# A fused attention and mixture-of-experts block on one core: one masking product per score tile, one maximum and one exponent per tile, and several steps put in another order

## The chip, the cores and the metric

The kernel runs on one core of one Trainium2 chip. The metric is the time of one execution on the device in microseconds (us); lower is better. The engines are called PE (TensorE), DVE (VectorE), ACT (ScalarE), POOL (GpSimd) and SP (SyncE, which only issues transfers here).

## What is computed

`x` and `ctx_2048` are 32 sequences of 64 tokens with 256 features. One block of a network is applied to them, with two gates (cut):

```python
# attention: keys and values are the 64 context rows of the same sequence and 64 rows made of x
q, k_new, v_new = xn @ wq.T, xn @ wk.T, xn @ wv.T            # xn = layernorm(x)
k, v = concat([ctx, k_new]), concat([ctx, v_new])            # per sequence, 128 rows
attn = softmax(q @ k.T / sqrt(256)) @ v @ wo.T
x = x + tanh(g_xattn) * attn
# feed-forward on xf = layernorm(x), 2048 tokens, 8 experts of width 176, the best 2 of each token
probs = softmax(xf @ gate_w.T);  top_p, top_i = top_k(probs, 2)
y = sum over the two experts of top_p * proj_e(silu(fc1_e(xf)) * fc2_e(xf))
y = y + sigmoid(xf @ shared_gate.T) * shared_proj(silu(shared_fc1(xf)) * shared_fc2(xf))   # width 704
x = x + tanh(g_ffn) * y
```

All is in float32. The kernel splits each matmul operand into a high and a low half (`_hi`, `_lo`) and multiplies three pairs of halves, hi x hi, hi x lo, lo x hi. So ACT makes each high half (a copy) and DVE the low one (a subtraction), and only then may PE go on: PE, ACT, DVE, PE is the chain of nearly every step.

## The kernel before

The 2048 tokens are four chunks (`c` = 0 to 3, `LAST` = 3) of four tiles (`j` = 0 to 3) of 128 tokens, that is two sequences a tile. Every engine has its own program, a list of steps written out by hand in order; each engine goes through its list strictly, and semaphores join them. What stands ahead of a step on its engine therefore sets when it can start.

**Attention** (lines 641 to 682 on PE, 960 to 1000 on ACT, 1380 to 1425 on DVE). For tile j of chunk c PE does `scores(c, j)`: six products of 256 columns into bank 4 or 5. The 256 columns are the keys of both sequences of the tile, so that half of what is computed belongs to the other sequence. `row_max` on DVE takes the maximum of each half of the rows over the keys of their own sequence, in two instructions (`own_keys`), and `exps` on ACT does the same with two exponent instructions, each with an instruction that reads the sum; the other sequence's places in `PR` stay at the zeros that were written once at the start. Then come `values` (12 products), `probs_t` (two transposes), `probs_hi` and `probs_lo`, `v_hi` and `v_lo`, and `attend` (six products; the second waits for `v_lo`, the third for `probs_lo`), `residual` and `aggregate`. Between these stand the steps of the next chunk (`first_norm`, `project`: its queries and keys, in bank 3) and of the last ones (`second_norm`, `router`, `logits`; `two_best`, `counts`, `route` and `slots`, which find for each token and expert a place in the sorted list; `scatter` on POOL writes rows there).

For a chunk c > 1, `slots(c - 2)` stands on DVE between `residual(c, 0)` and `v_lo(c, 1)`, and reads what `route(c - 2)` put into bank 7. In chunk 0 `ln1_stats(2)` stands ahead of `v_lo(0, 0)`; it needs the third chunk of `x`.

**Start** (lines 603 to 620, 922 to 935, 1323 to 1347): constants and weights are loaded and split; PE runs 18 transposes of a constant (`warm`) between the first steps.

**Shared feed-forward** of chunks 0 to 2 (`fc`, `pj`) comes next, then the **experts**: 39 tiles of 128 sorted rows, in a loop written out (`e_step`).

**End** (lines 816 to 824, 1549 to 1558): the shared feed-forward of chunk 3 in six blocks, `fc` (12 products of 512 columns; six in block 4) and `pj` (12 products of 256 columns; eight in block 4), with `s_silu`, `s_mult`, `s_hi`, `s_lo` between them. Meanwhile the partial sums come back from memory, and `combine(0)` to `combine(7)` add them: 0, 2, 4, 7 on DVE, 1, 3, 5, 6 on POOL. `s_last` adds chunk 3's shared part, and results are stored. Chunk 2's partial sums are loaded last; `combine(6)` and `combine(7)` are theirs.

Of the kernel before, what the change touches and what calls it, by code (L numbers as in the profile page):

```python
# [111 lines left out]
def build(nc, x, ctx_t, wa, sw, ew, rw, gates, consts, rconsts, out):  # L112
    with ExitStack() as stack:
# [316 lines left out]
        def _(pe):  # L430
# [95 lines left out]
            def attend(c, j):  # L526
# [1222 lines left out]
```

## Time and profile before

| | |
|---|---|
| time, median of 3 runs (range) | 295.76 us (294.89 to 295.84) |
| the profiled execution: its time, its span | 294.28 us, 292.5 us |
| busy in the span: PE, DVE, ACT, POOL | 272.9, 213.9, 170.7, 136.1 us |
| start and attention | to about 114 us |
| shared feed-forward of chunks 0 to 2 | about 114 to 183 us |
| the 39 expert tiles | about 183 to 265 us |
| shared feed-forward of chunk 3 and the stores | 265 us to the end |

The span runs from the first to the last instruction; the time of an execution lies 1.8 us above it. PE's products are pipelined and their ends are modelled, so waits of PE are best read from the starts of its products.

### The profile page before, as it was taken

The numbers are of one execution on the slowest core, as the hardware profiler recorded it, in microseconds if no ns is written. First come the engines' busy times: TensorE is split into PE (matmuls) and PEld (weight loads), VectorE is DVE, ScalarE is ACT, GpSimd is POOL, SyncE is SP. The second block draws the span as 40 slices with busy tenths as digits, with TensorE's granted clock in tenths as the row PEclk, the third lists the DMA queues.
The fourth block names the chain that finished last, engine by engine and source line by source line (L and its number), as shares of the span: only waits on it lengthen the run. The fifth ranks groups of instructions, "written<-read, shape, count | busy, mean of one in ns | idle before, by whom it ended". The sixth has DMA issues, their size and how long they took to land.

```text
span 292.5 us, 5859 instructions
## 1 busy us (share of the span) xinstructions
PE 272.9 (93%) x1777; PEld 245.7 (84%) x1777; DVE 213.9 (73%) x694; ACT 170.7 (58%) x401; POOL 136.1 (47%) x161
## 2 busy tenths in 40 slices
PE   3998899999899899999999999899999999999992
PEld 3887789789778677888788888899999999998882
DVE  6867776979869759768776767868778777763285
ACT  2775678687566567473335446566666667654240
POOL 2420831441784427453450000068778778776141
PEclk9999999999999999999999999999999999999999
DMA  6470244221136112544425744368888888756796
GB/s 194 190 256 2 73 149 141 72 80 50 38 91 242 74 40 85 186 144 125 150 76 182 247 140 145 131 113 134 136 141 134 136 139 137 116 69 72 291 354 217
DMA packets 25022, 40.18 MB, mean 137 GB/s; under 512 B 2976, under 2 KB 18976, under 8 KB 24992
## 3 DMA queue, kind: packets, MB, share of 16 engines
q1 hardware_dynamic: 16272, 27.43, 29.1%
q0 software_dynamic: 7152, 9.57, 19.4%
q10 hardware_dynamic: 1568, 2.80, 2.7%
q8 instruction: 15, 0.25, 0.4%
q14 instruction: 15, 0.12, 0.2%
HBM read 22.68 MB, written 17.11 MB: 136 GB/s over the span
## 4 chain that ended last, share of the span: by engine, by line
PE 57%; DVE 23%; issue 7%; ACT 6%; DMA 3%; POOL 1%; SPq 0%; DVEq 0%; ACTq 0%; POOLq 0%
PE bank L437 43%; PE bank L702 8%; DVE ew_lo L1097 4%; DMA xn_all<-x_dram 3%; PE bank L801 3%; PE bank L755 3%; DVE work L1453 2%; ACT ew_hi L830 2%; DVE xt_lo L1097 2%; ACT sh_hi L830 2%; DVE neg_max L1145 2%; DVE sh_lo L1097 2%; DVE ln_stats L1108 1%; DVE work L1168 1%; ACT work L862 1%
## 5 line engine op out<-in xcount | busy, mean ns | idle before, releaser
L1650 POOL DMA_INDIRECT y_d<-work,dest_of_slot x39 | 60.5, 1552 | 56.2 <-DVE dest_of_slot L1504 54.7
L437 PE MATMUL bank<-ew_hi,xt_hi 128*128 (+2 forms) x172 | 53.9, 323 | 1.4 <-DVE xt_lo L1097 0.7
L437 PE MATMUL bank<-ew_lo,xt_hi 128*128 (+2 forms) x172 | 51.7, 301 | 0.0
L437 PE MATMUL bank<-ew_hi,xt_lo 128*128 (+1 forms) x133 | 40.5, 305 | 0.0
L1610 POOL DMA_INDIRECT xs_d<-xn_all,slot_of_pair x32 | 33.3, 1042 | 10.1 <-issue 7.3
L1097 DVE TENSOR_TENSOR xt_lo<-bank,xt_hi 128x256 fp32r<-128x256 f32 (+2 forms) x90 | 35.5, 397 | 3.2 <-ACT xt_hi L830 2.0
L437 PE MATMUL bank<-xt_hi,sw_hi 128*128 128x512 f32 x88 | 34.8, 395 | 0.2 <-DVE work L1453 0.2
L437 PE MATMUL bank<-xt_lo,sw_hi 128*128 128x512 f32 x88 | 34.5, 392 | 0.0
L437 PE MATMUL bank<-xt_hi,sw_lo 128*128 128x512 f32 x88 | 34.3, 390 | 0.0
L830 ACT ACTIVATE xt_hi<-bank 128x256 fp32r<-128x256 f32 (+1 forms) x90 | 32.7, 409 | 2.4 <-PE bank L801 1.1
L437 PEld LDWEIGHTS bank<-ew_hi,xt_hi 128*128 128x128 f32 (+1 forms) x172 | 32.4, 189 | 2.0 <-DVE xt_lo L1097 0.9
L437 PE MATMUL bank<-ew_hi 128*128 128x256 f32 (+1 forms) x100 | 30.8, 314 | 3.4 <-DVE ew_lo L1097 2.0
L437 PEld LDWEIGHTS bank<-ew_lo,xt_hi 128*128 128x128 f32 (+1 forms) x172 | 32.7, 190 | 0.1
L1097 DVE TENSOR_TENSOR ew_lo<-bank,ew_hi 128x512 fp32r<-128x512 f32 (+1 forms) x41 | 22.6, 580 | 13.2 <-ACT ew_hi L830 13.1
L830 ACT ACTIVATE sh_hi<-work 128x512 fp32r<-128x512 f32 (+1 forms) x24 | 15.2, 632 | 28.8 <-DVE work L1453 25.2
L437 PE MATMUL bank<-ew_hi,ew_lo 128*128 128x256 f32 (+1 forms) x100 | 30.4, 310 | 1.5 <-DVE ew_lo L1097 1.5
L437 PE MATMUL bank<-ew_lo,ew_hi 128*128 128x256 f32 (+1 forms) x100 | 29.7, 304 | 0.6 <-DVE ew_lo L1097 0.2
L702 PE MATMUL bank<-sw_hi,sh_hi 128*128 128x256 f32 x96 | 27.2, 289 | 0.3 <-DVE work L1468 0.2
L830 ACT ACTIVATE ew_hi<-bank 128x512 fp32r<-128x512 f32 (+1 forms) x45 | 21.6, 518 | 9.3 <-PE bank L437 8.2
L702 PE MATMUL bank<-sw_lo,sh_hi 128*128 128x256 f32 x96 | 26.6, 282 | 0.0
L437 PEld LDWEIGHTS bank<-ew_hi,xt_lo 128*128 128x128 f32 x133 | 25.1, 188 | 0.0
L1490 DVE TENSOR_TENSOR work<-work,bank 128x176 f32<-128x176 f32 x39 | 13.1, 337 | 16.0 <-ACT work L1025 16.0
(161 smaller groups left out, 678.8 us busy)
## 6 DMA issues: line engine op xcount, KB each, us to landing
work<-xs_d SPq DMA_DIRECT2D x39, 136.0 KB, 2.5
weight_stage<-ew_dram SPq DMA_DIRECT2D x10, 486.5 KB, 3.7
y_d<-work SPq DMA_DIRECT2D x6, 512.0 KB, 3.9
work<-ctx_t_dram SPq DMA_DIRECT2D x4, 512.0 KB, 3.3
ew_hi<-y_d SPq DMA_DIRECT2D x4, 512.0 KB, 8.1
ew_hi<-y_d ACTq DMA_DIRECT2D x4, 512.0 KB, 7.0
xn_all<-x_dram SPq DMA_DIRECT2D x3, 512.0 KB, 6.6
xs_d<-pad_row SPq DMA_DIRECT2D x9, 136.0 KB, 2.0
```

The costliest lines, as they stand in the source:

```text
L437: last = nc.tensor.matmul(dst, a, b, start=(n == 0), stop=(n == len(pairs) - 1))
L702: last = nc.tensor.matmul(B[4 + t][:, 0:D], h[:, t * P:(t + 1) * P], w, start=(j == 0 and n == 0), stop=(j == S_FULL and n == len(parts) - 1))
L755: last = nc.tensor.transpose(rows_bank(n)[:, k * P:(k + 1) * P], EX[:, w, k * P:(k + 1) * P], ident)
L801: last = nc.tensor.transpose(B[4 + v][:, i * P:(i + 1) * P], EH[:, v, i * P:(i + 1) * P], ident)
L830: return nc.scalar.activation(dst, src, ACT.Copy, scale=scale)
L862: nc.scalar.activation(XA[:, j, :], XNR[:, c * TPC + j, :], ACT.Identity, bias=nb1[:, j:j + 1], scale=rs1[:, j:j + 1]).then_inc(a_xn, 1)
L1097: return nc.vector.tensor_tensor(dst, src, hi.bitcast(F32), ALU.subtract)
L1145: last = nc.vector.tensor_reduce(nmx[r, j % 2:j % 2 + 1], own_keys(B[4 + j % 2], b), mybir.AxisListType.XY, ALU.max, negate=True)
L1453: nc.vector.tensor_tensor(SHF[0:rows, j % 2, :], STH[0:rows, j % 2, :], h2, ALU.mult).then_inc(v_h, 1)
L1490: nc.vector.tensor_tensor(EH[:, u % 2, 0:F_E], ETH[:, u % 2, :], B[2 + u % 2][:, F_E:2 * F_E], ALU.mult)
L1610: nc.gpsimd.indirect_dma_start(out=xs_d, out_offset=bass.IndirectOffsetOnAxis(ap=POS[:, i, n:n + 1], axis=0), in_=XN[:, n, :], in_offset=N ...
L1650: nc.gpsimd.indirect_dma_start(out=y2_d, out_offset=bass.IndirectOffsetOnAxis(ap=IX[:, n:n + 1], axis=0), in_=EY[:, n % 4, :], in_offset=None,
```

## The change

- **Scores.** A seventh product is added to each `scores`: `SIDES` holds ones where row and token are of the same sequence, `OTHERS` holds -1e28 at the keys of the other sequence. It adds a number far down to the scores of the other sequence and zero to the own ones. So `row_max` and `exps` are one instruction each over all 256 columns. Both tiles are written once at the start; the zeros of `PR` go.
- **Slots.** `slots(c - 2)` moves behind `aggregate(c, 0)`, `route(c - 2)` behind `attend(c, 1)` and, for chunks 0 and 1, into bank 4. `scatter` is put behind `rstd2` on POOL.
- **Chunk 2.** `attend(2, 2)` moves behind `project(3, 3)`, its `residual` behind `project_lo(3, 3)`.
- **Chunks 0 and 1.** `ln1_stats(2)` goes behind `row_max(0, 2)`, `project_lo(1, 0)` ahead of `residual(0, 0)`, and the two halves of `first_norm(2)` stand one ahead of each of the first two `scores` of chunk 1.
- **Start.** 13 warming transposes instead of 18; `weight_lo(2)` and `(3)` ahead of `ln1_stats(1)`; `cached_hi(0)` behind `project_hi(0, 0)`; the load of the router's weights later.
- **End.** `fc` and `pj` of chunk 3 in another order; `combine(6)` goes from POOL to DVE, and `combine(7)` ahead of `s_last`.

The diff, cut to its core:

```diff
+        SIDES = EW[0][:, 9216:9216 + P]
+        OTHERS = EW[0][:, 9216 + P:9216 + 3 * P]
...
@@ PE @@
                 if j == 0:
-                    waits += [(0, v_qk, 4 * c + 4), (0, g_ct, c + 1)]
+                    waits += [(0, v_qk, 4 * c + 4), (0, g_ct, c + 1), (0, v_far, 1)]
...
-                              for m in range(KD) for a, b in THREE], waits)
+                              for m in range(KD) for a, b in THREE] + [(SIDES, OTHERS)], waits)
...
-                if j == 1 and c > 1:
-                    waits = waits + [(0, v_pos, c - 1)]
...
-                bank, o = (B[1], 0) if c == LAST else (B[7], D)
+                bank, o = (B[1], 0) if c == LAST else (B[7], D) if c == LAST - 1 else (B[4], 0)
...
             first_norm(0, 0)
-            warm(4)
             first_norm(0, 1)
-            warm(4)
+            warm(3)
...
+                if c == 1:
                     first_norm(c + 1, 0)
+                    scores(c, 0)
                     first_norm(c + 1, 1)
+                    scores(c, 1)
...
                 values(c, 1)
-                if c > 1:
-                    route(c - 2)
...
                 attend(c, 1)
+                if c > 1:
+                    route(c - 2)
...
-                attend(c, 2)
+                if c != LAST - 1:
+                    attend(c, 2)
                 values(c, 3)
                 probs_t(c, 3)
                 if c < LAST:
                     project(c + 1, 3)
+                if c == LAST - 1:
+                    attend(c, 2)
...
             fc(LAST, 1)
+            pj(LAST, 0)
+            fc(LAST, 2)
+            fc(LAST, 3)
+            pj(LAST, 1)
+            fc(LAST, 4)
+            fc(LAST, 5)
             for j in range(2, S_BLK):
-                if j < S_FULL:
-                    pj(LAST, j - 2)
-                fc(LAST, j)
-            for j in range(S_FULL - 2, S_BLK):
                 pj(LAST, j)
@@ ACT @@
-                for b in range(2):
-                    r = slice(b * SEQ, (b + 1) * SEQ)
-                    last = nc.scalar.activation(PR[r, j % 2, :, b, :], own_keys(B[4 + j % 2], b),
-                                                ACT.Exp, bias=nmx[r, j % 2:j % 2 + 1], accum_out=den[r, j:j + 1])
-                last.then_inc(a_exp, 1)
+                nc.scalar.activation(PR[:, j % 2, :, :, :].rearrange("p x s n -> p (x s n)"), B[4 + j % 2][:, 0:2 * P],
+                                     ACT.Exp, bias=nmx[:, j % 2:j % 2 + 1], accum_out=den[:, j:j + 1]).then_inc(a_exp, 1)
...
             weight_hi(1)
-            cached_hi(0)
             weight_hi(2)
             weight_hi(3)
-            for i in range(4):
+            project_hi(0, 0)
+            cached_hi(0)
+            for i in range(1, 4):
                 project_hi(0, i)
-            first_apply(1, (0, 1))
...
-            first_apply(1, (2, 3))
+            first_apply(1)
@@ DVE @@
-                for b in range(2):
-                    r = slice(b * SEQ, (b + 1) * SEQ)
-                    last = nc.vector.tensor_reduce(nmx[r, j % 2:j % 2 + 1], own_keys(B[4 + j % 2], b),
-                                                   mybir.AxisListType.XY, ALU.max, negate=True)
-                last.then_inc(v_mx, 1)
+                nc.vector.tensor_reduce(nmx[:, j % 2:j % 2 + 1], B[4 + j % 2][:, 0:2 * P], AX_X, ALU.max, negate=True).then_inc(v_mx, 1)
...
+                far = nc.vector.memset(OTHERS.rearrange("p (x s n) -> p x s n", x=2, s=2)[r, :, 1 - b, :].bitcast(F32), FAR)
```

What DVE has around `slots(0)` in chunk 2 before (L1172 ends `residual(2, 0)`, L1259 to L1264 is `slots(0)`, the rows behind it are `v_lo(2, 1)`, `second_lo(1, 1)`, `probs_lo(2, 1)` and `project_lo(3, 1)`):

```order
L1172 BN_STATS ln2_stats<-work 128x6
L1259 TENSOR_TENSOR work<-work,bank7 128x32
L1260 TENSOR_REDUCE work<-work 128x4
L1259 TENSOR_TENSOR work<-work,bank7 128x32
L1260 TENSOR_REDUCE work<-work 128x4
L1261 TENSOR_SCALAR payload<-work,tanh_gates 128x4x2
L1262 SCALAR_TENSOR_TENSOR slot_of_pair<-work 128x2x4
L1264 COPY work<-work 128x8
L1097 TENSOR_TENSOR ew_lo<-bank2,ew_hi 128x512
L1097 TENSOR_TENSOR xt_lo<-bank0,xt_hi 128x2x256
L1097 TENSOR_TENSOR ew_lo<-bank1,ew_hi 128x256
L1135 SCALAR_TENSOR_TENSOR sh_lo<-bank3,sh_hi 128x512
```

And in the changed kernel, from the same `residual(2, 0)` (L1190) to the first instruction of `slots(0)` (L1277):

```order
L1190 BN_STATS ln2_stats<-work 128x6
L1119 TENSOR_TENSOR ew_lo<-bank2,ew_hi 128x512
L1119 TENSOR_TENSOR xt_lo<-bank0,xt_hi 128x2x256
L1119 TENSOR_TENSOR ew_lo<-bank1,ew_hi 128x256
L1157 SCALAR_TENSOR_TENSOR sh_lo<-bank3,sh_hi 128x512
L1165 TENSOR_REDUCE neg_max<-bank5 128x1
L1186 SCALAR_TENSOR_TENSOR work<-bank7,softmax_scale,xn2_all 128x256
L1190 BN_STATS ln2_stats<-work 128x6
L1196 BN_AGGR ln2_mean_var<-ln2_stats 128x2 x2
L1277 TENSOR_TENSOR work<-work,bank4 128x32
```

The seven instructions of `slots(0)` now stand behind `residual(2, 1)` and `aggregate(2, 0)`, and each maximum is one instruction.

What DVE has in chunk 0 from the first maxima on, before (L1108 and L1112 are `ln1_stats(2)`):

```order
L1145 TENSOR_REDUCE neg_max<-bank5 64x1 x2
L1108 BN_STATS ln1_stats<-xn2_all 128x6 x4
L1112 BN_AGGR ln1_mean_var<-ln1_stats 128x2 x4
L1097 TENSOR_TENSOR ew_lo<-bank2,ew_hi 128x512
L1097 TENSOR_TENSOR ew_lo<-bank0,ew_hi 128x256
L1097 TENSOR_TENSOR xt_lo<-bank6,xt_hi 128x2x256
L1097 TENSOR_TENSOR xt_lo<-bank7,xt_hi 128x2x256
L1145 TENSOR_REDUCE neg_max<-bank4 64x1 x2
```

And in the changed kernel (L1130 and L1134 are `ln1_stats(2)`):

```order
L1165 TENSOR_REDUCE neg_max<-bank5 128x1
L1119 TENSOR_TENSOR ew_lo<-bank2,ew_hi 128x512
L1119 TENSOR_TENSOR ew_lo<-bank0,ew_hi 128x256
L1119 TENSOR_TENSOR xt_lo<-bank6,xt_hi 128x2x256
L1119 TENSOR_TENSOR xt_lo<-bank7,xt_hi 128x2x256
L1165 TENSOR_REDUCE neg_max<-bank4 128x1
L1130 BN_STATS ln1_stats<-xn2_all 128x6 x4
L1134 BN_AGGR ln1_mean_var<-ln1_stats 128x2 x4
L1119 TENSOR_TENSOR ew_lo<-bank2,ew_hi 128x512
L1119 TENSOR_TENSOR ew_lo<-bank1,ew_hi 128x256
L1157 SCALAR_TENSOR_TENSOR sh_lo<-bank3,sh_hi 128x512
L1180 RECIPROCAL softmax_scale<-softmax_sum 128x2
```

The statistics moved behind five steps, and `project_lo(1, 0)` (L1157) stands ahead of `residual(0, 0)`.

The end of DVE's list before (L1453 is `s_mult`, L1097 `s_lo`, L1440 `combine`, L1483 `s_last`):

```order
L1453 TENSOR_TENSOR work<-work,bank0 64x512
L1097 TENSOR_TENSOR sh_hi<-work,sh_hi 64x512
L1453 TENSOR_TENSOR work<-work,bank3 128x512
L1440 TENSOR_TENSOR xn2_all<-ew_hi 128x2x256
L1097 TENSOR_TENSOR sh_lo<-work,sh_hi 128x512
L1483 SCALAR_TENSOR_TENSOR xn2_all<-bank4,shared_gate,xn2_all 128x256
L1483 SCALAR_TENSOR_TENSOR xn2_all<-bank5,shared_gate,xn2_all 128x256
L1483 SCALAR_TENSOR_TENSOR xn2_all<-bank6,shared_gate,xn2_all 128x256
L1483 SCALAR_TENSOR_TENSOR xn2_all<-bank7,shared_gate,xn2_all 128x256
L1440 TENSOR_TENSOR xn2_all<-ew_hi 128x2x256
```

And in the changed kernel (L1482 `s_mult`, L1119 `s_lo`, L1469 `combine`, L1512 `s_last`):

```order
L1482 TENSOR_TENSOR work<-work,bank0 64x512
L1482 TENSOR_TENSOR work<-work,bank3 128x512
L1469 TENSOR_TENSOR xn2_all<-ew_hi 128x2x256
L1119 TENSOR_TENSOR sh_hi<-work,sh_hi 64x512
L1469 TENSOR_TENSOR xn2_all<-ew_hi 128x2x256
L1119 TENSOR_TENSOR sh_lo<-work,sh_hi 128x512
L1469 TENSOR_TENSOR xn2_all<-ew_hi 128x2x256
L1512 SCALAR_TENSOR_TENSOR xn2_all<-bank4,shared_gate,xn2_all 128x256
L1512 SCALAR_TENSOR_TENSOR xn2_all<-bank5,shared_gate,xn2_all 128x256
```

`combine(6)`, which was POOL's, now stands ahead of the last `s_lo`, and `combine(7)` behind it and ahead of `s_last`.

## Rows read from the trace of the kernel before

**Rows 1.** Page, the chain that ended last: share of the span by engine.

```profile
PE 57%; DVE 23%; issue 7%; ACT 6%; DMA 3%; POOL 1%; SPq 0%; DVEq 0%; ACTq 0%; POOLq 0%
```

**Rows 2.** Stretches: length, then busy PE, PEld, DVE, ACT, POOL; clock; DMA; GB/s.

```profile
20.00:45.00 25.00, 22.01 (x156) 19.79 (x154) 17.68 (x49) 17.04 (x46) 9.01 (x20) 1.00 0.28 95
65.00:90.00 25.00, 23.68 (x166) 21.06 (x165) 20.78 (x75) 15.96 (x43) 15.53 (x26) 1.00 0.27 94
90.00:112.00 22.00, 19.93 (x130) 16.98 (x129) 16.68 (x76) 14.13 (x34) 8.46 (x19) 1.00 0.24 91
```

**Rows 3.** Timeline of PE: start, length, instruction, in brackets the wait ahead.

```profile
18.63 0.28 PE L437 MATMUL bank<-ew_lo,ew_hi 128*128 128x256 f32 x1
18.75 0.27 PE L437 MATMUL bank<-ew_hi,ew_lo 128*128 128x256 f32 x1
```

**Rows 4.** Timeline of PE, products that came late in attention.

```profile
24.46 0.38 PE L437 MATMUL bank<-ew_hi 128*128 128x256 f32 x1 [1.45 <-DVE ew_lo L1097]
...
30.76 0.50 PE L437 MATMUL bank<-xt_hi,ew_hi 128*128 128x512 f32 x1 [0.90 <-DVE sh_lo L1135]
...
41.20 0.63 PE L445 MATMUL bank<-consts_sb,work 128*128 128x128 f32 x4 [0.57 <-ACT work L862]
...
77.43 0.39 PE L437 MATMUL bank<-ew_hi,ew_lo 128*128 128x256 f32 x1 [0.55 <-DVE ew_lo L1097]
...
87.88 0.36 PE L437 MATMUL bank<-sw_hi,sh_hi 128*128 128x256 f32 x1 [0.58 <-issue]
...
97.89 0.35 PE L437 MATMUL bank<-ew_hi 128*128 128x256 f32 x1 [0.73 <-DVE work L1264]
...
99.32 0.38 PE L437 MATMUL bank<-ew_hi,ew_lo 128*128 128x256 f32 x1 [0.55 <-DVE ew_lo L1097]
```

**Rows 5.** Timeline of DVE in chunks 0 and 2.

```profile
21.86 1.41 DVE L1108 BATCH_NORM_STATS2 ln_stats<-xn_all 128x6 f32<-128x256 f32 x4 [1.48 <-DMA xn_all<-x_dram]
...
74.22 0.17 DVE L1259 TENSOR_TENSOR work<-work,bank 128x32 f32<-128x32 f32 x1
...
75.76 0.68 DVE L1097 TENSOR_TENSOR ew_lo<-bank,ew_hi 128x512 fp32r<-128x512 f32 x1
...
76.96 0.41 DVE L1097 TENSOR_TENSOR ew_lo<-bank,ew_hi 128x256 fp32r<-128x256 f32 x1
...
81.18 1.02 DVE L1097 TENSOR_TENSOR ew_lo<-bank,ew_hi 128x512 fp32r<-128x512 f32 x2 [1.45 <-ACT ew_hi L830]
```

**Rows 6.** Groups by form: busy us, mean ns of one, idle before them.

```profile
L891 ACT ACTIVATE work<-bank,neg_max 64x128 f32<-64x128 f32 x32 | 11.6, 363 | 17.2 <-DVE neg_max L1145 17.0
...
L1145 DVE TENSOR_REDUCE neg_max<-bank 64x1 f32<-64x128 f32 x32 | 9.1, 285 | 0.4
...
L1097 DVE TENSOR_TENSOR ew_lo<-bank,ew_hi 128x256 fp32r<-128x256 f32 x16 | 6.6, 413 | 0.0
...
L830 ACT ACTIVATE ew_hi<-bank 128x256 fp32r<-128x256 f32 x16 | 6.1, 380 | 0.0
L891 ACT ACTIVATION_READ_ACCUMULATOR work<-bank,neg_max 64x1 f32 x32 | 6.0, 187 | 0.0
```

**Rows 7.** Timeline of the start, PE and ACT.

```profile
4.22 2.39 PE L592 MATMUL bank<-consts_sb 128*128 128x128 f32 x10 [4.22 <-DMA consts_sb<-consts_dram]
...
8.98 0.60 PE L592 MATMUL bank<-consts_sb 128*128 128x128 f32 x4
...
16.97 1.09 ACT L862 ACTIVATE work<-xn_all,ln_bias,ln_rstd 128x256 f32<-128x256 f32 x2 [0.67 <-POOL ln_bias L1570]
```

**Rows 8.** Timeline of the end: POOL, DVE, PE and ACT's transfer queue.

```profile
285.10 1.27 POOL L1660 TENSOR_TENSOR xn_all<-ew_hi 128x512 f32<-128x512 f32 x1 [2.28 <-DMA ew_hi<-y_d]
...
285.19 1.72 DVE L1097 TENSOR_TENSOR sh_lo<-work,sh_hi 128x512 fp32r<-128x512 f32 x1
...
286.97 0.39 PE L702 MATMUL bank<-sw_hi,sh_lo 128*128 128x256 f32 x1 [1.25 <-DVE sh_lo L1097]
...
289.76 0.39 ACTq L1090 DMA_DIRECT2D out_dram<-xn_all  x1
```

More of the change, by code:

```diff
@@ L44 @@
 PAD = 1e6
+FAR = -1e28
 SLOT_TILES = (N_TOK * TOP + N_E * (P - 1)) // P
@@ L641, in _ @@
             for c in range(1, N_CH):
-                if 0 < c < LAST:
+                if c == 1:
                     first_norm(c + 1, 0)
+                    scores(c, 0)
                     first_norm(c + 1, 1)
-                scores(c, 0)
-                scores(c, 1)
+                    scores(c, 1)
+                else:
+                    if c < LAST:
+                        first_norm(c + 1, 0)
+                        first_norm(c + 1, 1)
+                    scores(c, 0)
+                    scores(c, 1)
                 values(c, 0)
@@ L1327, in _ @@
             nc.vector.memset(SX, 0.0)
-            nc.vector.memset(WK[:, 4608:5120], 0.0)
+            nc.vector.memset(EW[0][:, 9216:9216 + 3 * P].bitcast(F32), 0.0).then_inc(v_far0, 1)
+            dve.wait_ge(v_far0, 1)
+            for b in range(2):
+                r = slice(b * SEQ, (b + 1) * SEQ)
+                nc.vector.memset(SIDES[r, r].bitcast(F32), 1.0)
+                far = nc.vector.memset(OTHERS.rearrange("p (x s n) -> p x s n", x=2, s=2)[r, :, 1 - b, :].bitcast(F32), FAR)
+            far.then_inc(v_far, 1)
             ln1_stats(0, (0, 1))
@@ L1338, in _ @@
             weight_lo(1)
-            ln1_stats(1)
-            project_lo(0, 0)
             weight_lo(2)
             weight_lo(3)
+            project_lo(0, 0)
+            ln1_stats(1)
             project_lo(0, 1)
@@ L1355, in _ @@
             row_max(0, 1)
-            ln1_stats(2)
             v_lo(0, 0)
@@ L1361, in _ @@
             row_max(0, 2)
+            ln1_stats(2)
             v_lo(0, 1)
             probs_lo(0, 1)
+            project_lo(1, 0)
             residual(0, 0)
-            project_lo(1, 0)
             row_max(0, 3)
@@ L1411, in _ @@
                     ln1_stats(c + 2)
+                if c > 1:
+                    slots(c - 2)
                 v_lo(c, 2)
@@ L1418, in _ @@
                     project_lo(c + 1, 2)
-                residual(c, 2)
+                if c != LAST - 1:
+                    residual(c, 2)
                 v_lo(c, 3)
@@ L1423, in _ @@
                     project_lo(c + 1, 3)
+                if c == LAST - 1:
+                    residual(c, 2)
                 residual(c, 3)
@@ L1549, in _ @@
             for j in range(S_BLK):
-                s_mult(LAST, j)
-                if j in (3, 5):
-                    combine((0, 4)[j // 5])
+                if j < S_FULL:
+                    s_mult(LAST, j)
+                if j == 3:
+                    combine(0)
+                if j == S_FULL - 1:
+                    s_mult(LAST, S_FULL)
+                    combine(4)
+                if j == S_FULL:
+                    combine(6)
                 s_lo(LAST, j)
@@ L1555, in _ @@
                     combine(2)
+            combine(7)
             for t in range(TPC):
                 s_last(t)
-            combine(7)
         @block.gpsimd
@@ L1660, in combine @@
                 nc.gpsimd.tensor_tensor(XNR[:, t, :], Y2[0][:, t, :], Y2[1][:, t, :], ALU.add).then_inc(g_c2, 1)
-            for n in (1, 3, 5, 6):
+            for n in (1, 3, 5):
                 combine(n)
-def own_keys(bank, b):
-    rows = bank[b * SEQ:(b + 1) * SEQ, 0:2 * P]
-    return rows.rearrange("p (x s n) -> p x s n", x=2, s=2)[:, :, b, :]
 def layout(inputs):
```

51 lines of the change are left out of this document (32 added, 19 removed).

## Prediction

> **What bounds the kernel now.** I read the chain that ended last first: more than half of it is PE, a quarter DVE, hardly any transfers [rows 1]. Then the stretches. Through attention PE is busy for most of each stretch, but not all: 25.00 less 22.01, 25.00 less 23.68 and 22.00 less 19.93 leave 2.99, 1.32 and 2.07, together 6.4 us of visible idleness in 72 us [rows 2]. DVE is busy for 20.78 of 25 us in chunk 2, so it is nearly full as well. The granted clock reads 1.00 there, the level of 2.4 GHz. Products of 256 columns follow each other by 0.12 us [rows 3]; this pitch, not the 0.28 of one, is the price of a product where PE is the bound. The waits themselves are few and long: seven of them make 5.3 us [rows 4]. Behind most stands DVE. A wait in the middle of an `attend` shows short, because the ends of products are modelled: in `attend(3, 1)` the first product starts at 97.89 after 0.73, the third should follow 0.24 later, and stands at 99.32 [rows 4], so 0.73 + 1.19 = 1.9 us are lost there where the rows in brackets show 1.28. From this I conclude that attention is PE's work plus a handful of waits on DVE, and that an edit is worth what it does to those waits, less what it adds to PE. The shared blocks and expert tiles are not touched; whatever attention gains is passed on through them, since the steps there hang on each other and no transfer of theirs is tied to a fixed time.
>
> **The added product.** One product in each of 16 tiles, by 0.12 [rows 3]: 16 x 0.12 = 1.9 us, all on PE and all paid, as PE is the bound. Its weight load lies under the products beside it, as those of the other six do. The two tiles are written at the start while DVE would wait for x; I cost that at nothing, and at 0.5 at most, which is the length of the write that goes.
>
> **Maxima and exponents.** Before, two maxima of 285 ns and two exponents of 363 ns, each with a read of 187 ns [rows 6]. After, one maximum over 256 elements and one exponent with one read. No row shows either. From below the maximum costs what one costs now, 285; from above twice that, 570; the nearest row is DVE's subtraction of 256 elements out of a bank, 413. So I take 0.41 and save 0.57 - 0.41 = 0.16 a tile. The exponent: from below 363, from above 726; the copy of 256 elements takes 380, and I take 0.45, a little above it because an exponent of 128 takes 363 already. ACT saves 0.73 + 0.37 - 0.45 - 0.19 = 0.46 a tile, less some overlap, say 0.4. That is 2.6 us of DVE and 6 us of ACT, which are worth something only at PE's waits: the four maxima of a chunk stand in DVE's list ahead of the low halves that PE waits for. For the waits that no reordering touches I take 0.7 in all.
>
> **Order, wait by wait.**
> - Chunk 0, product at 24.46 (wait 1.45) [rows 4]. `v_lo(0, 0)` is late because `ln1_stats(2)` ahead of it sat until 21.86 for x, 1.48 us, and then took 1.4 [rows 5]. It goes behind five steps. What is late next is ACT: `cached_hi(0)` comes later, so POOL's split of it and POOL's `rstd1(1)` behind that come later, and ACT already waits for them at 16.97 [rows 7], with the exponents queued behind. I take 1.0 of the 1.45.
> - Chunk 0, 30.76 (0.90) [rows 4]: `project_lo(1, 0)` no longer stands behind `residual(0, 0)`, but the statistics (1.4) now stand ahead of it. I take 0.6.
> - Chunk 1, 41.20 (0.57) [rows 4]: PE waits for ACT's normalised tiles; `scores(1, 0)` is put into that wait. 0.5.
> - Chunk 2, 77.43 [rows 4]: DVE ends `probs_lo(2, 1)` at 76.96 + 0.41 = 77.37 and PE starts 0.06 later, so DVE holds it. `slots(0)` fills DVE from 74.22 to 75.76, 1.54 us [rows 5]. It leaves this place and lands behind `aggregate(2, 0)`, where DVE idles for 1.45 before 81.18 [rows 5]: that idle time hides it, and were it gone, `v_lo(2, 2)` would be late by up to 1.5. Between 0.55 (shown) and 1.54 I take 1.2.
> - Chunk 3's start, 87.88 (0.58) [rows 4]: `attend(2, 2)` fills the wait for `project_lo(3, 3)`. But both residuals of tiles 2 and 3 now stand ahead of `row_max(3, 0)` on DVE, and its exponents behind that. 0.5 here, and 0.3 given back below.
> - Chunk 3, 97.89 and 99.32 (1.9 as above) [rows 4]: here even the first product waits for the end of `slots(1)`, L1264. With bank 7 free and `slots(1)` elsewhere, I take 1.6, less the 0.3: 1.3.
> - Start: `first_norm(0, 1)` loses four transposes ahead of it, 0.60 for four [rows 7], and DVE's idle time before the statistics is filled. This gain mostly meets the later POOL steps just described. I take 0.4.
>
> Waits: 1.0 + 0.6 + 0.5 + 1.2 + 0.5 + 1.3 + 0.4 + 0.7 = 6.2. Less the products: 6.2 - 1.9 = 4.3 off attention.
>
> **The end.** PE waits 1.25 us for the last `s_lo`, which takes 1.72 where the subtraction starts 0.09 after POOL's `combine(6)` and lies under it to its end [rows 8]. Two things change. The chain of block 5 starts one `pj` earlier (12 products by 0.12, 1.4 us), and `combine(6)` is DVE's. But it stands ahead of `s_lo` and needs chunk 2's partial sums, which are there at 285.10 [rows 8]. So DVE does `combine(6)` from 285.1 and `s_lo` from about 285.8, done by 286.5 instead of 286.9: 0.4 for PE. Then `combine(7)` no longer follows `s_last`: the last store of ACT is issued at 289.76 before [rows 8] and may be issued about 1.0 earlier, 0.4 from PE and 0.6 for one `combine` less. I take 0.9. From below it is -0.3, if the stores now issued earlier push those sums back; from above 1.4.
>
> **Sum.** 4.3 + 0.9 = 5.2 off. Two of my entries are cautious, since I charge the statistics and POOL's delay in full while the waits they would cause overlap; carrying the steps of chunks 2 and 3 forward one behind the other gave me 1 us more there. I set 6.0. The profiled execution took 294.28, so 288.3. The median of the runs shown is 295.76, 1.5 above it; the same share off it gives 289.7.
>
> **Rivals.**
> - *The wait moves on.* DVE does the same steps, only later: `slots` reappears before `values(c, 2)`, the statistics before `project(1, 1)`. For it speaks DVE's 20.78 of 25 [rows 2]; against it the 1.45 of idleness right behind [rows 5]. Half the waits: 3.1 - 1.9 + 0.9 = 2.1 off, 293.6.
> - *Nothing of the waits is won, the products are paid.* If POOL and ACT replace DVE as the late one wherever DVE gets earlier (exponents of chunk 3 late by two residuals, `rstd1(1)` late at the start), 1.9 is added and 0.9 saved at the end: 1.0 slower, 296.8. It decides as soon as less than 1.0 us of the 6.2 is won. It ends on the slower side.
> - *The low clock at the start.* The first ten transposes take 2.39, 0.24 each, and four later ones 0.60 [rows 7], ends included: PE starts at the lower pace, the level of 1.2 GHz, and has the full one when the first large products begin. Five transposes fewer leave it idle longer before them. Should PE enter them at the lower level, each of the 24 products of 512 columns (0.24 at the full pace, twice 0.12) costs up to 0.24 more: +5.8, which leaves 0.2 off, 295.6, no change. Against it: 13 transposes and the two `first_norm` remain, with the same gaps of well under a microsecond. The Trainium skill ("TensorE: Matmul & The Clock Gate", The HAM clock gate) says that the throttled clock is the default and that activity releases it, which speaks against taking warming work away; the rows agree in the slow first ten. By it the time would be that same 295.6.
> - *Every wait named goes.* 1.45 + 0.90 + 0.57 + 1.5 + 0.58 + 1.9 + 0.7 + 0.8 = 8.4, less 1.9, plus 1.4 at the end: 7.9 off, 287.8; somewhat more, if the lighter ACT also shortens waits that these rows do not show, 286.5.
>
> **Chances.** My forecast, 4.5 to 7.5 off: 0.50. Every wait goes, more than that: 0.15. The wait moves on, 1 to 4.5 off: 0.18. Within 0.3% (0.9 us, about what a measurement of this kernel can tell from none), the clock's case among it: 0.07. Slower: 0.10. So faster 0.83. The likeliest case's own range is 288.2 to 291.2. The whole range reaches from 286.5 to the rival where the wait moves on, 293.9; the ends leave out the slower and unchanged cases.
>
> **What would show it.** Right: L437's successor has 16 more products of 256 columns; one `TENSOR_REDUCE` of 128 partitions a tile near 0.41 and one exponent near 0.45; in the timeline of PE no wait over 0.5 us in the `attend` of tile 1 in chunks 2 and 3; `slots` behind `aggregate` with DVE still idle before `v_lo(c, 2)`; attention over about 4 to 5 us earlier, and the same distance kept through the experts; the last `s_lo` at 0.7 instead of 1.72. Wrong: new waits of PE at `probs_t(0, 0)` or `attend(3, 0)`, a maximum near 0.57, a slow pace in the first products of 512 columns, or a last `s_lo` that starts after 286.5 less the shift.

## The result: 286.28 us, 9.2 us less than before

| | before | after |
|---|---|---|
| time, median (range), 4 runs each | 295.47 us (294.89 to 295.84) | 286.28 us (286.08 to 287.11) |
| ratio to before, 95% interval | | 0.9696 [0.9669, 0.9723] |
| the profiled execution: its time, its span | 294.28, 292.5 us | 286.08, 284.3 us |
| busy in the span: PE, DVE, ACT, POOL | 272.9, 213.9, 170.7, 136.1 us | 271.9, 209.7, 164.2, 134.6 us |

The kernel is faster, as predicted, but by 9.2 us and not by 6; 286.28 lies 0.2 under the range's lower end. (One execution of all that follow, of 292.56 us in "two masking products", was in a slow state, over 1.5% above the fastest of its kernel, and its ratio leaves it out.) The chain that ended last, page of the changed kernel, answers to [rows 1]:

```profile
PE 81%; DVE 7%; DMA 5%; ACT 4%; issue 2%; ACTq 0%; DVEq 0%
```

DVE's part fell from 23% to 7%: its steps no longer lie between PE's. The same stretches as [rows 2], in the changed kernel (length; busy PE, PEld, DVE, ACT, POOL; clock; DMA; GB/s):

```profile
20.00:45.00 25.00, 24.73 (x179) 22.84 (x178) 18.86 (x48) 18.45 (x42) 9.03 (x20) 1.00 0.43 146
...
65.00:90.00 25.00, 24.54 (x182) 22.46 (x181) 19.94 (x71) 13.92 (x33) 15.55 (x26) 1.00 0.31 102
90.00:112.00 22.00, 21.10 (x120) 17.00 (x119) 18.02 (x60) 13.93 (x27) 11.98 (x19) 1.00 0.28 93
```

PE stands idle for 0.27 + 0.46 + 0.90 = 1.6 us of these 72, where it was 6.4. The groups that answer to [rows 6]:

```profile
L906 ACT ACTIVATE work<-bank,neg_max 128x256 f32<-128x256 f32 x16 | 7.5, 471 | 10.3 <-DVE neg_max L1165 10.3
L1165 DVE TENSOR_REDUCE neg_max<-bank 128x1 f32<-128x256 f32 x16 | 6.5, 412 | 0.3 <-PE bank L441 0.3
L906 ACT ACTIVATION_READ_ACCUMULATOR work<-bank,neg_max 128x1 f32 x16 | 3.1, 194 | 0.0
```

I had taken 0.41 for the maximum and 0.45 for the exponent; they take 412 and 471 ns. The products that are still late, in the timeline of PE, answer to [rows 4]:

```profile
86.79 0.38 PE L441 MATMUL bank<-ew_lo,ew_hi 128*128 128x256 f32 x1 [0.41 <-issue]
...
91.21 0.39 PE L441 MATMUL bank<-ew_lo,ew_hi 128*128 128x256 f32 x1
91.54 0.39 PE L441 MATMUL bank<-ew_hi,ew_lo 128*128 128x256 f32 x1
...
92.49 0.38 PE L586 MATMUL bank<-work 128*128 128x32 f32 x2 [0.21 <-ACT work L906]
...
96.45 0.38 PE L441 MATMUL bank<-ew_hi 128*128 128x256 f32 x1 [0.37 <-ACT ew_hi L848]
```

They are all in chunk 3, in `attend(3, 0)`, `(3, 1)`, `route(1)` and `attend(3, 2)`; outside it the timeline shows only one wait, of 0.27 at 37.26, `scores(1, 0)`. None of the seven of [rows 4] is left at its size. Now the end, DVE and ACT's transfer queue, against [rows 8]:

```profile
277.82 0.69 DVE L1469 TENSOR_TENSOR xn_all<-ew_hi 128x512 f32<-128x512 f32 x1 [0.60 <-DMA ew_hi<-y_d]
278.43 0.68 DVE L1119 TENSOR_TENSOR sh_lo<-work,sh_hi 128x512 fp32r<-128x512 f32 x1
279.03 0.69 DVE L1469 TENSOR_TENSOR xn_all<-ew_hi 128x512 f32<-128x512 f32 x1
...
281.35 0.46 ACTq L1112 DMA_DIRECT2D out_dram<-xn_all x1
```

The first row is `combine(6)`, which waits 0.60 for its sums, as foreseen. The last `s_lo` takes 0.68 where it took 1.72, PE waits 0.38 for it where it waited 1.25 (row below), and from its end to the issue of the last store it is 281.35 - 279.11 = 2.24 us where it was 289.76 - 286.91 = 2.85: the `combine` less that was foreseen.

```profile
279.17 0.39 PE L718 MATMUL bank<-sw_hi,sh_lo 128*128 128x256 f32 x1 [0.38 <-DVE sh_lo L1119]
```

**A ruler.** Every kernel below was read at the same five steps of PE: the first product of `scores(0, 0)`, of `project(1, 1)`, the first transpose of `first_norm(3, 0)` (which opens chunk 2), the first products of `scores(3, 0)` and of `fc(0, 2)`; and from there to the end of the execution. Differences, from the timelines of PE, in us:

| kernel | to project(1, 1) | to chunk 2 | to scores(3, 0) | to fc(0, 2) | attention | rest |
|---|---|---|---|---|---|---|
| before | 13.40 | 33.13 | 23.99 | 26.71 | 97.2 | 179.7 |
| changed | 10.38 | 32.05 | 22.33 | 26.25 | 91.0 | 178.4 |

By this ruler attention gives 6.2, its start 0.7 (`scores(0, 0)` at 16.70 instead of 17.36), and the rest 1.3: together 8.2, the difference of the two profiled executions (294.28 - 286.08). The remaining 1.0 of the medians' 9.2 is in which executions were profiled. The ruler leaves out the start, which varies between executions of one and the same start code: the first large product stands between 9.2 and 11.2 us in those of the kernels below that share the changed start, depending on when the constants land. Medians carry that noise. In attention the stretches do not: to `project(1, 1)` the seven kernels that share its steps take 10.38 to 10.41. The rest does vary: it is 178.2 to 179.2 in the eleven kernels with the changed end and 179.7, 180.3 and 180.6 in the three with the old one. The two groups do not touch, and their means lie 1.6 apart.

### The profile page after: what moved, and what is told of

It reads as the page before. It is cut to its first block, busy times and chain, and to the rows that moved or that the text cites. A ratio compares the mean times of both kernels' runs of the same rounds, so it can differ in the third digit from the quotient of the medians.

```text
span 284.3 us, 5839 instructions
## 1 busy us (share of the span) xinstructions
PE 271.9 (96%) x1788; PEld 246.7 (87%) x1788; DVE 209.7 (74%) x683; ACT 164.2 (58%) x369; POOL 134.6 (47%) x160
## 4 chain that ended last, share of the span: by engine, by line
PE 81%; DVE 7%; DMA 5%; ACT 4%; issue 2%; ACTq 0%; DVEq 0%
PE bank L441 62%; PE bank L718 7%; DMA ew_hi<-y_d 3%; PE bank L449 3%; PE bank L817 3%; PE bank L771 3%; DVE work L1482 2%; ACT sh_hi L848 1%; DVE sh_lo L1119 1%; DMA consts_sb<-consts_dram 1%; PE bank L528 1%; ACT ew_hi L848 1%; DVE ew_lo L1119 1%; PE bank L598 1%; ACT work L1028 1%
## 5 line engine op out<-in xcount | busy, mean ns | idle before, releaser
L1119 DVE TENSOR_TENSOR xt_lo<-bank,xt_hi 128x256 fp32r<-128x256 f32 (+2 forms) x90 | 35.6, 397 | 3.6 <-ACT xt_hi L848 2.4
L441 PE MATMUL bank<-ew_hi 128*128 128x256 f32 (+1 forms) x116 | 33.3, 307 | 0.6 <-ACT ew_hi L848 0.6
L1119 DVE TENSOR_TENSOR ew_lo<-bank,ew_hi 128x512 fp32r<-128x512 f32 (+1 forms) x41 | 22.8, 582 | 10.9 <-ACT ew_hi L848 9.6
```

The source lines that it names most:

```text
L441: last = nc.tensor.matmul(dst, a, b, start=(n == 0), stop=(n == len(pairs) - 1))
L1119: return nc.vector.tensor_tensor(dst, src, hi.bitcast(F32), ALU.subtract)
```

## Experiments

Twelve kernels, five rounds each, in three groups of four with runs of the kernel before beside them. "Undone" means the changed kernel with one part as it was before. The groups ran on three chips, where the kernel before took 295.54, 294.88 and 295.27, and the changed kernel was not run again; so a difference of under about 0.7 us between a median here and 286.28 says little. The stretches are read from one profiled execution of each kernel.

| kernel | median us (range) | ratio to before [95%] | to project(1, 1) | to chunk 2 | to scores(3, 0) | to fc(0, 2) | attention |
|---|---|---|---|---|---|---|---|
| scores undone | 292.46 (290.18 to 294.09) | 0.9882 [0.9834, 0.9931] | 11.39 | 33.84 | 22.92 | 27.38 | 95.5 |
| fused scores alone | 293.03 (292.41 to 293.69) | 0.9907 [0.9874, 0.994] | 12.78 | 32.29 | 23.30 | 26.39 | 94.8 |
| slots undone | 287.53 (287.11 to 288.38) | 0.9726 [0.9692, 0.9759] | 10.38 | 32.06 | 22.86 | 26.24 | 91.5 |
| end undone | 288.28 (287.83 to 289.25) | 0.9755 [0.9722, 0.9787] | | | | | 91.0 |
| start and chunks 0, 1 undone | 289.96 (289.32 to 290.3) | 0.9825 [0.9805, 0.9845] | 12.54 | 32.27 | 22.39 | 26.28 | 93.5 |
| two masking products | 288.33 (287.96 to 292.56) | 0.9777 [0.9755, 0.9799] | 10.76 | 32.45 | 22.84 | 26.51 | 92.6 |
| two exponents | 289.15 (287.99 to 290.56) | 0.9802 [0.9775, 0.9828] | 10.99 | 32.94 | 22.35 | 26.86 | 93.1 |
| two maxima | 288.5 (287.29 to 288.86) | 0.9764 [0.9739, 0.9788] | 10.71 | 32.40 | 22.42 | 26.98 | 92.5 |
| chunk 2 undone | 286.79 (286.54 to 287.66) | 0.9727 [0.9702, 0.9752] | 10.39 | 32.03 | 22.79 | 26.34 | 91.6 |
| eighteen transposes | 287.62 (286.77 to 288.71) | 0.9744 [0.9716, 0.9772] | 10.41 | 32.03 | 22.39 | 26.41 | 91.2 |
| chunk 3 undone | 288.74 (287.21 to 290.52) | 0.9786 [0.9746, 0.9826] | 10.40 | 32.02 | 22.34 | 29.26 | 94.0 |
| slots and chunk 3 undone | 287.9 (287.0 to 288.65) | 0.9758 [0.9733, 0.9783] | 10.41 | 32.02 | 22.83 | 26.92 | 92.2 |

### The fused scores, undone and alone

Six products, two maxima and two exponents a tile in the otherwise changed kernel:

```diff
-                              for m in range(KD) for a, b in THREE] + [(SIDES, OTHERS)], waits)
+                              for m in range(KD) for a, b in THREE], waits)
```

(with `row_max` and `exps` in two instructions, as the minus lines of the change show them), and the opposite, the kernel before with only the added product, one maximum and one exponent.

> The changed kernel with the scores as before: six products, two maxima and two exponents a tile, everything else kept. Theory O (order: the gain is the waits on DVE that the new order takes away, the one product and one maximum and exponent about pay for each other): 285.5 to 287.5, within 1 us of the changed kernel, since 1.9 us of products go and some 2 us of waits come back. Rival F (the shorter path through maximum and exponent is most of the gain, because PE waits for it at every tile): 290 or more.

> The kernel before with only the added product, one maximum and one exponent. Theory O: 294.5 to 296.5, no change to speak of. Rival F: 291 or less.

Undone, it costs 4.5 us in attention; alone it gives 2.5. Neither is the small matter that I had made of it. (The median grew by 6.2, more than the 4.5: in the profiled execution `scores(0, 0)` starts 1.96 later too, 1.7 of it because the first transpose does, at 6.22 instead of 4.53.) The product costs PE 1.5 to 1.9 (next experiment); with 1.9 the shorter steps on DVE and ACT are worth 4.5 + 1.9 = 6.4 in the new order and 2.5 + 1.9 = 4.4 in the old one. All four stretches pay: 1.0, 1.8, 0.6 and 1.1 from "scores undone" to "changed". What a tile saves is seen on ACT; first the kernel with scores undone, then the changed one:

```profile
26.53 0.36 ACT L908 ACTIVATE work<-bank,neg_max 64x128 f32<-64x128 f32 x1 [1.53 <-DVE neg_max L1170]
26.80 0.19 ACT L908 ACTIVATION_READ_ACCUMULATOR work<-bank,neg_max 64x1 f32 x1
27.00 0.36 ACT L908 ACTIVATE work<-bank,neg_max 64x128 f32<-64x128 f32 x1
27.27 0.19 ACT L908 ACTIVATION_READ_ACCUMULATOR work<-bank,neg_max 64x1 f32 x1
27.48 0.87 ACT L848 ACTIVATE ew_hi<-bank 128x512 fp32r<-128x512 f32 x2
```

```profile
92.98 0.47 ACT L906 ACTIVATE work<-bank,neg_max 128x256 f32<-128x256 f32 x1 [0.63 <-DVE neg_max L1165]
93.35 0.19 ACT L906 ACTIVATION_READ_ACCUMULATOR work<-bank,neg_max 128x1 f32 x1
```

From the first exponent to the end of the last read it is 27.27 + 0.19 - 26.53 = 0.93 against 93.35 + 0.19 - 92.98 = 0.56: 0.37 less on ACT, and 0.57 - 0.41 = 0.16 less on DVE, 0.53 a tile, 8.5 in sixteen. The steps queued behind them (`v_hi`, `probs_hi`, `v_lo`, `probs_lo`) can come earlier by that. Set beside the 8.5, PE gains 6.4 in the new order.

### The price of the product, and each instruction by itself

The product twice (`+ [(SIDES, OTHERS), (SIDES, OTHERS)]`), which leaves the probabilities as they are; then only the exponents in two, or only the maxima in two, each with the product kept:

```diff
-                nc.vector.tensor_reduce(nmx[:, j % 2:j % 2 + 1], B[4 + j % 2][:, 0:2 * P], AX_X, ALU.max, negate=True).then_inc(v_mx, 1)
+                for b in range(2):
+                    r = slice(b * SEQ, (b + 1) * SEQ)
+                    last = nc.vector.tensor_reduce(nmx[r, j % 2:j % 2 + 1], own_keys(B[4 + j % 2], b),
+                                                   mybir.AxisListType.XY, ALU.max, negate=True)
+                last.then_inc(v_mx, 1)
```

> The changed kernel with the masking product given twice in each tile: the number put on the other sequence is twice as far down, the own scores unchanged. If PE is the bound throughout attention: 16 x 0.12 = 1.9 us more, 288.2. If PE's waits on ACT and DVE take it in: under 1 us more.

> The changed kernel with its product and its one maximum, but the exponents again in two instructions. Theory A (what the fusion gives is ACT's shorter exponents: ACT copies the high halves behind them): most of the 6 us that undoing the fusion cost, less the 1.9 of products, comes back here: 291 or more. Theory V (it is DVE's maximum): within 1.5 us of the changed kernel, 287.8 or less. If both are needed at once: in between, with this and the next adding up to less than 8 us.

> The changed kernel with its product and its one exponent, but the maximum again in two instructions. Theory A: within 1.5 us of the changed kernel, 287.8 or less. Theory V: 291 or more.

One more product costs 1.5 in attention and 2.05 in the medians, around the 16 x 0.12 = 1.9 of the prediction: PE is the bound nearly throughout. The one exponent is worth 2.1 and the one maximum 1.5 in attention (2.9 and 2.2 in the medians). Both count; added up 3.6, less than the 6.4 that both at once are worth by the sum above, so the second one to be lost costs more than the first. That the changed kernel has a little slack behind each tile, which the first uses up, would explain it and was not tested.

### The order: start and chunks 0 and 1

The start, `ln1_stats(2)`, `project_lo(1, 0)` and `first_norm(2)` as before, the rest as changed; in DVE's list:

```diff
-                ln1_stats(2)
-                project_lo(1, 0)
+                project_lo(1, 0)
```

> The changed kernel with the start and chunks 0 and 1 in the order of before (18 warming transposes, weights, statistics, first_apply, first_norm(2)); the fused scores, slots and the end kept. Theory N (each reordering acts on its own wait): 289 or more, since the stretch from the first scores to project(1, 1) took 10.4 us against 12.8 with the fusion alone, and the start some 0.5 more. Rival M (the fusion has opened room on DVE and ACT, and with it a reordering is worth little, as that of slots was): 287.3 or less.

It costs 2.5 in attention, 2.2 of it before `project(1, 1)`. `scores(0, 0)` starts at 18.22 instead of 16.70; counted from the first transpose (4.95 and 4.53) that is 13.27 instead of 12.17, so the start costs 1.1 more. The waits come back where they were, those of chunk 0 smaller than in [rows 4], in the timeline of PE:

```profile
25.12 0.39 PE L441 MATMUL bank<-ew_hi 128*128 128x256 f32 x1 [1.11 <-DVE ew_lo L1114]
30.76 0.50 PE L441 MATMUL bank<-xt_hi,ew_hi 128*128 128x512 f32 x1 [0.34 <-DVE sh_lo L1152]
41.21 0.63 PE L449 MATMUL bank<-consts_sb,work 128*128 128x128 f32 x4 [0.56 <-ACT work L875]
```

### Slots, and the middle of chunk 3

First `slots`, `route` and `scatter` where they stood; then, with those as changed, chunk 3's middle steps in the old order; then both. The second is a part of the change that neither the list of it nor the prediction named: in chunk 3 `probs_t(3, 1)` goes ahead of `second_norm(2, 1)`, and `probs_hi(3, 1)` ahead of `second_hi(2, 1)` and `exps(3, 2)`. The second edit on PE:

```diff
                 values(c, 1)
-                if c == LAST:
-                    probs_t(c, 1)
                 second_norm(c - 1, 1)
-                if c < LAST:
-                    probs_t(c, 1)
+                probs_t(c, 1)
```

> The changed kernel with slots, route and scatter where they were before. Theory O: 2.5 to 3.5 us slower than the changed kernel (289), and PE waits again in attend(2, 1) and attend(3, 1). Rival F: under 1 us slower, because the lighter maxima and exponents have given DVE the time.

> The changed kernel with the order of chunk 3's middle steps as before (the second half of chunk 2's second norm ahead of probs_t(3, 1) on PE, and the same on ACT and DVE), slots and route where the change has them. Theory Q (this reordering, not the move of slots, took the 1.9 us of waits in attend(3, 1)): the stretch behind scores(3, 0), 26.25 us in the changed kernel, grows by 0.8 to 1.5, and the median goes to about 287.4. Theory R (both share one wait, so either alone takes it): the stretch stays within 0.3 us, as it did with slots alone undone, and only the kernel with both undone shows the loss.

> The changed kernel with slots, route and scatter where they stood before, and chunk 3's middle steps in the order of before too. Slots alone undone cost 0.5 us in chunk 2 and nothing behind scores(3, 0). Theory Q: as the kernel with chunk 3 alone undone, plus that 0.5: stretch behind scores(3, 0) up by 0.8 to 1.5, median about 288. Theory R: here alone the stretch grows, by 1.0 to 1.9, median 288 to 288.5. A third reading (the fused maximum and exponent alone took that wait away): the stretch grows by under 0.4 in both kernels, and the median stays near the 287.5 of slots alone undone.

Slots undone costs 0.5, all in chunk 2; I had given it 1.2 there and much of chunk 3's 1.3. Both undone cost 1.2. But chunk 3 alone undone costs 3.0 in its profiled execution, more than both: none of the readings written down. In the timeline of PE of that execution:

```profile
90.70 0.28 PE L441 MATMUL bank<-ew_hi 128*128 128x256 f32 x1
92.53 0.39 PE L441 MATMUL bank<-ew_hi 128*128 128x256 f32 x1 [1.56 <-ACT ew_hi L845]
...
93.32 0.40 PE L441 MATMUL bank<-ew_hi,ew_lo 128*128 128x256 f32 x1 [0.28 <-DVE ew_lo L1112]
...
94.86 0.68 PE L441 MATMUL bank<-xt_hi,router 128*72 128x512 f32 x1
95.34 0.63 PE L441 MATMUL bank<-xt_lo,router 128*72 128x512 f32 x1
95.77 0.63 PE L441 MATMUL bank<-xt_hi,router 128*72 128x512 f32 x1
```

`attend(3, 1)` waits 1.56 for its probabilities' high half, which stands on ACT behind `exps(3, 2)` and `second_hi(2, 1)`. And then PE is slow: the router's products follow each other by 0.43 to 0.48, and by 0.24 in the changed kernel. The same stretches of the same kernel show why in the clock column:

```profile
92.50:94.00 1.50, 1.19 (x6) 0.98 (x7) 1.09 (x3) 0.37 (x2) 0.00 (x0) 0.85 0.00 0
94.00:95.00 1.00, 1.00 (x7) 1.00 (x7) 0.57 (x2) 0.19 (x2) 0.00 (x0) 0.50 0.00 0
95.00:96.00 1.00, 1.00 (x4) 0.62 (x4) 0.90 (x6) 0.00 (x0) 0.29 (x2) 0.50 0.34 117
96.00:97.00 1.00, 1.00 (x4) 0.71 (x4) 0.86 (x5) 0.14 (x1) 0.84 (x3) 0.52 0.38 145
97.00:98.00 1.00, 1.00 (x11) 1.00 (x10) 0.08 (x1) 0.46 (x1) 0.69 (x3) 1.00 0.05 10
```

After that wait the granted clock fell to 0.50, the level of 1.2 GHz, for about 3.4 us: 1.50 x 0.15 x 2 = 0.45 of the first row's, then 94.00 to about 96.96. From the third product of `attend(3, 1)` to the first of `values(3, 2)` (96.62 here, 93.90 in the changed kernel) it takes 3.30 us instead of 2.36. With 0.16 more in the first two products of `values(3, 2)` the pace costs 0.94 + 0.16 = 1.1. So of the 3.0 some 1.6 is the wait, 1.1 the pace, and 0.3 comes later. In none of the other traces of this study does the clock fall in attention. That the wait brought the fall on is the order of the two in one trace, not tested by itself.

The fall came in some executions of this kernel only. The profiled one has a mean granted clock of 0.994, as 3.4 us at half the clock in 287.7 give; those of 287.21, 287.94 and 288.01 us have 0.997, 1.000 and 1.000, too high for such a fall. (The other two, 290.22 and 290.52, have 0.994 as well.) So without the fall this kernel takes about what the one with both undone takes, 287.9, and its trace less the pace leaves 3.0 - 1.1 = 1.9 beside the 1.2 of both. What stays is smaller than the 3.0: with `slots` moved, the order in chunk 3 is worth 1.9; with `slots` in its old place, 1.2 - 0.5 = 0.7.

### Chunk 2

`attend(2, 2)` and its residual at their old places:

```diff
-                if c != LAST - 1:
-                    attend(c, 2)
+                attend(c, 2)
```

> The changed kernel with attend(2, 2) and its residual where they stood before. Theory N (each move in the order took one wait away, at its own place): the wait of about 0.6 us before scores(3, 0) comes back, the stretch from chunk 2's start to scores(3, 0), 22.33 us in the changed kernel, grows by 0.4 to 0.8, and the median by the same, to about 286.8. Theory M (once the fused maximum and exponent have given DVE and ACT room, single moves are worth nothing): the stretch stays within 0.2 us, the median within 0.3 of 286.3. A gain of over 0.5 us would say that the move itself was a loss, by the two residuals that it puts ahead of row_max(3, 0).

The stretch to `scores(3, 0)` grows by 0.46, and the wait is there again; the median grows by 0.5, within what the chips differ by:

```profile
81.69 0.36 PE L441 MATMUL bank<-sw_hi,sh_hi 128*128 128x256 f32 x1 [0.59 <-issue]
```

### The warming transposes

```diff
+            warm(4)
             first_norm(0, 1)
-            warm(3)
+            warm(4)
```

> The changed kernel with eighteen warming transposes again, the rest of the start as changed. My rival of the low clock said that fewer of them risk a slower pace in the first large products; the trace of the changed kernel shows no such pace. If the five transposes taken away were only work, they cost up to 5 times 0.15 us, 0.75, when PE is what the start waits for, and nothing when it waits for DVE and the loads: 286.3 to 287.0. If they kept the clock up in some executions, the median with eighteen is below 286.3 and its spread narrower than a microsecond.

The time from the first transpose to the first product of 512 columns grows from 9.45 - 4.53 = 4.92 to 5.95, so 1.0 us, and the median by 1.3; the ten kernels with thirteen transposes take 4.52 to 5.03. It is more than I had written, since the extra ones run at the slow pace too:

```profile
7.98 1.06 PE L598 MATMUL bank<-consts_sb 128*128 128x128 f32 x4
8.83 1.06 PE L449 MATMUL bank<-consts_sb,work 128*128 128x128 f32 x4
9.68 1.06 PE L598 MATMUL bank<-consts_sb 128*128 128x128 f32 x4
```

### The end

`fc`, `pj` and the `combine`s of chunk 3 as before, `combine(6)` on POOL again (`for n in (1, 3, 5, 6)`).

> The changed kernel with the end as before (order of fc and pj, combine(6) on POOL, combine(7) last). Both theories: 0.9 to 1.2 us slower (287.2), the last s_lo again 1.7 long under POOL's combine. Rival at this place (the end is bound by the arrival of the partial sums and the stores): no change, 286.3.

The part behind `fc(0, 2)` grows from 178.4 to 180.3, and the median by 2.0. It is the collision with POOL that returns, at another victim. First DVE, then POOL, in the timeline of that kernel:

```profile
278.24 1.55 DVE L1464 TENSOR_TENSOR xn_all<-ew_hi 128x512 f32<-128x512 f32 x1
279.71 0.68 DVE L1114 TENSOR_TENSOR sh_lo<-work,sh_hi 128x512 fp32r<-128x512 f32 x1
...
277.94 1.30 POOL L1684 TENSOR_TENSOR xn_all<-ew_hi 128x512 f32<-128x512 f32 x1 [0.89 <-DMA ew_hi<-y_d]
```

`combine(4)` on DVE takes 1.55 under POOL's `combine(6)`, where a `combine` takes 0.69 alone, and `s_lo` behind it starts later by the difference; PE waits 0.91 for it. The same trace has a second collision of the kind: the `s_lo` ahead takes 1.66 from 275.94, under POOL's `combine(5)` (1.30 from 275.76), where it takes 0.69 in the changed kernel, and PE waits 0.51 there instead of 0.16.

## Why the prediction was right in kind and short in size

- **What bounds the kernel, and the added product.** Right. A second product costs 1.5 to 2.05 beside the 1.9 taken.
- **Durations.** Right: 412 and 471 ns for 0.41 and 0.45.
- **What they are worth.** This is the step that failed: "For the waits that no reordering touches I take 0.7 in all." I had worked out 2.6 us of DVE and 6 of ACT, and then let them count only at waits that rows in brackets show. Their worth is 6.4 with the new order and 4.4 with the old one. The sum of all lateness shows it: take the distance of each start of PE in attention from the one before, less the pitch of the product before (0.12 for 256 columns, 0.23 for 512, 0.11 for a transpose). What is left over, in us, by the steps where most of it lies:

  | step | before | fused scores alone | scores undone | changed |
  |---|---|---|---|---|
  | `values(0, 1)` | 1.70 | 1.63 | 1.01 | 0.00 |
  | `project(1, 1)` and `(1, 2)` | 1.23 | 0.66 | 0.96 | 0.33 |
  | `probs_t(1, 0)` and `attend(1, 1)` | 1.20 | 0.00 | 1.48 | 0.00 |
  | `attend(2, 1)` | 1.51 | 0.50 | 0.86 | 0.00 |
  | `probs_t(3, 0)` and `attend(3, 0)` | 0.93 | 0.53 | 1.82 | 0.89 |
  | `attend(3, 1)` | 2.19 | 1.80 | 1.81 | 0.79 |
  | all of attention | 15.1 | 10.7 | 13.4 | 6.9 |

  The seven waits of [rows 4] are the seven largest of these gaps, but only 6.7 of the 15.1. The fused scores alone take 4.4 away, 2.0 of it at the very steps that I had credited to the order, the other 2.4 at steps that no reordering touches, above all `probs_t(1, 0)` and `attend(1, 1)`; for those I had counted 0.7 in all. With the new order alone (scores undone) the waits move on, to `project(1, 2)`, `probs_t(1, 0)` and `probs_t(3, 0)`, and only 1.7 go. The 8.1 us that go with both are the 6.2 of the ruler and the 1.9 of the products. As idleness in windows over all of attention only 7.6 - 1.7 = 5.9 of the 8.1 were ever to be seen (first the kernel before, then the changed one):

```profile
17.00:115.00 98.00, 90.44 (x608) 78.83 (x607) 74.75 (x249) 67.61 (x167) 43.21 (x82) 1.00 0.28 97
```

```profile
16.00:108.00 92.00, 90.30 (x627) 80.66 (x627) 71.93 (x233) 60.92 (x135) 44.45 (x84) 1.00 0.32 109
```

  The rest lay inside runs of products whose modelled ends cover it. I had seen that in `attend(3, 1)` and had not carried it to the other fifteen tiles.
- **Chunks 0 and 1, start.** I took 1.0 + 0.6 up to `project(1, 1)`, where undoing costs 2.2, so most of the delay of ACT and POOL that I had charged did not come; and 0.5 in chunk 1, whose stretch grows by 0.2. These moves were undone together, and no run parts them. The start gave 0.7 at `scores(0, 0)`, and 1.0 counted from the first transpose (13.14 to 12.17), beside the 0.4 taken; the five transposes alone are worth that 1.0.
- **Chunks 2 and 3.** I took 1.2 + 1.3 for `slots` and what stands around `attend(3, 1)`; undone together with the order in chunk 3, which I had not named, they cost 1.2. Too much: the shorter scores already take 1.0 from `attend(2, 1)` and 0.4 from `attend(3, 1)` in the old order. `attend(2, 2)`: 0.5 taken, 0.46 measured.
- **The end.** 0.9 taken; undone 1.9 in the trace and 2.0 in the medians, 1.3 between the two profiled executions, 1.6 between the means of all traces. The mechanism (POOL's `combine(6)` beside DVE) was right. The extra stands at PE's wait for the last `s_lo`: I took 0.4 from it, and it went from 1.25 to 0.38; the `combine` less gave the 0.6 taken. Which of the block order and the move of `combine(6)` shortened the wait, these runs don't part.
- **Rivals.** None came true. The wait moves on: no, the new late products are small and in chunk 3. The low clock at the start: no, PE enters the large products at the full pace with thirteen transposes. Every wait goes, 7.9 off by my count, was nearest in size; even it counted the lighter ACT with little, and 6.9 of the 15.1 us of lateness are still there.

The parts don't add up: undone one at a time in the changed kernel they cost 4.5 + 2.5 + 1.2 + 0.5 in attention, 8.7 us, for a change that gained 6.2 there. They lean on each other, above all on the fused scores, whose loss costs 4.5 with the rest present and whose presence alone gives 2.5.

No experiment gave a median below 286.28; chunk 2 undone lies so near it (286.79) that only its stretch shows the loss.

## What to carry to other kernels

Where three engines hand each tile around in a ring, price a shorter instruction by its time in the ring times the number of tiles, and discount that (here 4.4 and 6.4 of 8.5 came), instead of looking for waits to set it against; the brackets of the timeline before showed 6.8 us in attention where 15.1 were late. The gaps between starts, less the pitch, are the sum that such an estimate has to fit into. Moves in the order of steps are worth what the rest of the ring leaves them: the order in chunk 3 was worth 1.9 with `slots` moved and 0.7 without, so undo them in pairs too. And look at the clock of each execution before a difference is put down to the order: 1.1 us here was not the edit's own.

## What had not been expected of the hardware

- Waits of PE of 1.56 and 0.28 us in the middle of dense work were followed by 3.4 us at the granted clock of 0.50, which added 1.1 us to their cost, in some executions of that kernel and not in others. In the kernel before, PE waited 1.45 at 24.46 [rows 4] and the clock stayed at 1.00 [rows 2].
- At the start the transposes follow each other by 0.21, though the granted clock reads 1.00 there. With eighteen of them in the changed order all run so, up to the first large product at 10.58; in the kernel before the last four took 0.60 together, ends included [rows 7], and follow by 0.11. The Trainium skill ("TensorE: Matmul & The Clock Gate", Part 1: The HAM clock gate) says that the number of slow products at a start differs from run to run of one kernel. The traces agree: of the ten kernels with the changed start and thirteen transposes, five (end, chunk 2, chunk 3, slots and chunk 3 undone, and two masking products) have the last transposes 0.11 apart, and the other five 0.21 nearly or quite to the end. No run here profiles one kernel twice.
- DVE's `combine` of 512 elements takes 0.69 alone and 1.55 under POOL's. The Trainium skill ("SBUF — State Buffer", SBUF: two separate sides) gives the reason as one pair of ports that only one of the two holds for a whole instruction. The trace agrees: the delay moves with POOL's instruction from `s_lo` to `combine(4)`, and in all three collisions DVE ends 0.54 to 0.55 after POOL does (286.91 after 286.37, 279.79 after 279.24, 277.60 after 277.06). `s_mult`, one of whose inputs is a bank, keeps its 0.69 under POOL's `combine(5)` in the changed kernel (275.00, under 274.43 to 275.73).
